# The FFN of a transformer and RWKV stack: products of split values against plain fp32 products

## The chip, the cores and the metric

The program runs on one core of one Trainium2 chip. The metric is the time on the device of one execution, in microseconds. The core has five engines with a program each: TensorE (PE), VectorE (DVE), ScalarE (ACT), GpSimd (POOL) and SyncE (SP, here only for DMAs). They run side by side and wait for each other on semaphores.

## The reference

Eight sequences of 1024 tokens with 256 channels go through four blocks, each with a layernorm before it and a residual after it: causal attention with rotary embedding, a gated FFN, an RWKV6 block, and the same FFN again. The FFN's weights are whole numbers from -127 to 127, scaled:

```python
x = x + _L0_attn_a_ref(_layernorm(x), Wq, Wk, Wv, Wo)
x = x + _L0_ffn_ref(_layernorm(x), w_gate, w_up, w_down)
x = x + _L0_attn_b_ref(_layernorm(x), ...)
x = x + _L0_ffn_ref(_layernorm(x), w_gate, w_up, w_down)
...
wg = w_gate.astype(x.dtype) * (1.0 / 127.0)
gate = jnp.einsum('bsd,hd->bsh', x, wg)
up = jnp.einsum('bsd,hd->bsh', x, wu)
h = jax.nn.silu(gate) * up
return jnp.einsum('bsh,dh->bsd', h, wd)
```

The hidden width is 768. All of it is fp32.

## The kernel before

A loop runs over the eight sequences (`b`, called batches here). In each, the stages follow one another: attention, first FFN (`ffn(1, ...)`, semaphore set 0), RWKV block, second FFN (`ffn(3, ...)`, set 1). Each engine has its own list, written out by hand, and each instruction is issued in that order. PSUM has eight banks; six of them (`RING`) are handed out in the order of one list, `psum_plan`, in which every product stands with the engine that empties its bank. `wait_bank` on PE waits until the product six places earlier has been emptied; `wait_filled` and `wait_emptied` are the waits of the other engines and of later steps.

An FFN works on halves `f` of 512 tokens and on tiles of 128 hidden rows: 12 tiles `e` for each sequence. For a tile, `gate_up` makes two products of 128x512 (`gu`, gate and up), each a sum over two chunks of 128 channels. ACT makes a tanh of the gate product (`turn`, L862), DVE adds one and multiplies by the gate (L1139) and then by the up product (L1144). `down` multiplies the hidden tiles by `wd` into 128x256 outputs, a sum over six tiles. Half of the down products stand in the middle of the tiles and half at the end.

The value operand of each product is split in two. `xh` is the input rounded to float32r, written by ACT (L846), and `xl` is the rest, written by DVE (L1126). In the same way `hh` is the rounded hidden tile, written by ACT (L853), and `hl` the rest, written by POOL (L683). PE takes both against the same float32r weights:

```python
for x in (xh, xl):
    w, v = wgu[:, c, rows], x[:, c, cols]
    last = mm(bank(b, f"gu{k}", 2 * e + r)[:, :], w, v, start=..., stop=...)
```

The hidden tiles stand in a ring: four places for `turn` (`TURNS`), ten or seven for `hh` and `hl` (`SLOTS`). The setup rounds the weights to float32r, subtracts that from the weights, and sets a flag if anything is left over (L504 to L516). PE loads it, and ahead of each FFN a branch chooses between these products and the same ones in plain fp32 (`general`).

Inside the first FFN stage PE also makes the second half of the attention's output projection (`out_proj(2)` and `out_proj(3)`, L1420) after tile 0, the transposes of the second half of the normed input (L1333), and at its end 16 transposes for what comes next. In the second, it makes four pieces of V for the next sequence (`v_item`, L1355) at the end.

Names: `xn` stands in the tile `attn`, `arena` is a large SBUF tile for most temporaries, `PB` are the PSUM banks. L1537 (`lora_item`) is the first product of the RWKV block; L1712 is its last one, L1525 its `mix` products.

Of the kernel before, what the change touches and what calls it, by code (L numbers as in the profile page):

```python
# [6 lines left out]
NB, T, D = 8, 1024, 256  # L7
# [56 lines left out]
SLOTS = {1: 10, 3: 7}  # L64
TURNS = 4
# [47 lines left out]
def psum_plan():  # L113
# [6 lines left out]
    def ffn(b, k):  # L120
        for f in (0, 1):
            for e in range(2 * NM):
                if f == 0 and k == 1 and e == 2:
                    add(b, "o", (2, 3), "dve")
                if f == 0 and e == 2 * SECOND_AT[k]:
                    add(b, f"ln{k}", (2, 3), "dve")
# [16 lines left out]
    for b in range(NB):  # L143
# [16 lines left out]
        add(b, "ln1", (0, 1), "dve")  # L160
# [47 lines left out]
        add(b, "ln3", (0, 1), "dve")  # L208
# [14 lines left out]
def build(nc, x_in, w_at, cs, b_vec, b_mat, ffn_w, consts, out):  # L223
    f32, bf16, i32, f32r = mybir.dt.float32, mybir.dt.bfloat16, mybir.dt.int32, mybir.dt.float32r
# [3 lines left out]
    with ctx:  # L228
# [19 lines left out]
        wgu = sb("wgu", [128, NC, 2 * HID], f32r)  # L248
        wd = sb("wd", [128, NM, D], f32r)
        wide_row = sb("wide_row", [128, 128])  # L250
        wide_flag = sb("wide_flag", [128, 1], i32)
# [39 lines left out]
        def rounded(name, first, shape):  # L291
            assert first + shape[1] * shape[2] <= ARENA
            return nc.alloc_sbuf_tensor_at(name, shape, f32r, offset=ARENA_AT + 4 * first)

# [16 lines left out]
        def ffn_tiles(k, first, hidden):  # L311
            return (rounded(f"xh{k}", first, [128, NC, T]), rounded(f"xl{k}", first + 2048, [128, NC, T]),
                    region(first + 4096, 512 * TURNS).rearrange("p (r t) -> p r t", r=TURNS),
                    rounded(f"hh{k}", hidden, [128, SLOTS[k], HALF]),
                    rounded(f"hl{k}", hidden + 512 * SLOTS[k], [128, SLOTS[k], HALF]))

        ffn_sets = {1: ffn_tiles(1, 0, 4096 + 512 * TURNS), 3: ffn_tiles(3, HIGH, HIGH + 4096 + 512 * TURNS)}
        assert HIGH + 4096 + 512 * (TURNS + 2 * SLOTS[3]) <= LAST

# [32 lines left out]
        s_split = sem("weights_split")  # L352
        s_raw = sem("raw_weights_moved")
        s_ones = sem("ones_stored")
        s_flag = sem("flag_moved")
# [31 lines left out]
        x_high = [sem("x_high1"), sem("x_high3")]  # L387
        h_high = [sem("h_high1"), sem("h_high3")]
        h_low = [sem("h_low1"), sem("h_low3")]
# [45 lines left out]
        NW = 2 * NC * HID + NM * D  # L435
        WF_AT, WR_AT, ONES_AT = 20 * 1024, 10 * 1024, 26 * 1024
        FLAG_AT = WF_AT - 1
        wf = arena[:, WF_AT:WF_AT + NW]
        gate, up = (wf[:, NC * HID * r:NC * HID * (r + 1)].rearrange("p (c n) -> p c n", c=NC) for r in (0, 1))
        down = wf[:, 2 * NC * HID:].rearrange("p (m n) -> p m n", m=NM)  # L440
        wr = rounded("wr", WR_AT, [128, 1, NW])
        ones = arena[96:99, ONES_AT:ONES_AT + 512].bitcast(bf16).rearrange("p (a n) -> p a n", a=1).broadcast_to([3, NH, T])
        with nc.Block() as block:
            @block.sync
            def _(sp):
# [32 lines left out]
                sp.wait_ge(s_split, 1)  # L478
                sp.dma_start(wgu[:, :, 0:HID].bitcast(f32), gate).then_inc(s_raw, 16)
                sp.dma_start(wgu[:, :, HID:2 * HID].bitcast(f32), up).then_inc(s_raw, 16)  # L480
                sp.dma_start(wd[:, :, :].bitcast(f32), down).then_inc(s_raw, 16)
                sp.wait_ge(s_split, 5)
                sp.dma_start(wide_row[0:1, :], arena[:, FLAG_AT:FLAG_AT + 1]).then_inc(s_flag, 16)
                sp.wait_ge(s_raw, 48)
# [15 lines left out]
            @block.vector  # L500
            def _(dve):
                dve.wait_ge(s_w, 16 * NLOAD)
                ai = arena[:, :].bitcast(i32)
                dve.tensor_copy(wf, ai[:, 0:NW]).then_inc(s_split, 1)  # L504
                dve.wait_ge(s_split, 1)
                dve.tensor_copy(wr[:, 0, :], wf).then_inc(s_split, 1)
                dve.wait_ge(s_split, 2)
                dve.tensor_tensor(arena[:, 0:NW], wf, wr[:, 0, :].bitcast(f32), ALU.subtract).then_inc(s_split, 1)
                dve.wait_ge(s_split, 3)
                dve.tensor_scalar(arena[:, 0:NW], arena[:, 0:NW], 0.0, None, ALU.not_equal).then_inc(s_split, 1)  # L510
                dve.wait_ge(s_split, 4)
                dve.reduce_max(arena[:, FLAG_AT:FLAG_AT + 1], arena[:, 0:NW], axis=AX.X).then_inc(s_split, 1)
                dve.wait_ge(s_flag, 16)
                dve.reduce_max(arena[0:1, WR_AT - 1:WR_AT], wide_row[0:1, :], axis=AX.X).then_inc(s_split, 1)
                dve.wait_ge(s_split, 6)
                dve.tensor_copy(wide_flag[0:1, :], arena[0:1, WR_AT - 1:WR_AT])  # L516
                dve.tensor_copy(causal[:, :], arena[:, 8192:8320])
                dve.tensor_copy(identb[:, :], ident[:, :]).then_inc(s_cast, 1)
# [22 lines left out]
        with nc.Block() as block:  # L541
# [49 lines left out]
            def _(pool):  # L591
# [22 lines left out]
                for b in range(NB):  # L614
# [65 lines left out]
                    def h_low_part(k, s, e):  # L680
                        _, _, turn, hh, hl = ffn_sets[k]
                        pool.wait_ge(h_high[s], 2 * NM * b + e + 1)
                        pool.tensor_tensor(hl[:, e % SLOTS[k], :], turn[:, e % TURNS, :], hh[:, e % SLOTS[k], :].bitcast(f32),  # L683
                                           ALU.subtract).then_inc(h_low[s], 1)
# [73 lines left out]
                    for e in range(2 * NM):  # L758
                        h_low_part(3, 1, e)

            @block.scalar
            def _(act):
# [27 lines left out]
                for b in range(NB):  # L790
# [48 lines left out]
                    def ffn(k, s):  # L839
                        xh, _, turn, hh, _ = ffn_sets[k]  # L840

                        def x_parts(ns):
                            for n in ns:
                                f, c = n // 2, n % 2
                                wait_filled(act, b, f"ln{k}", n)
                                act.activation(xh[:, c, HALF * f:HALF * f + HALF], bank(b, f"ln{k}", n)[:, :],  # L846
                                               ACT.Copy).then_inc(x_high[s], 1)

                        def h_part(e):
                            wait_emptied(act, b, f"gu{k}", 2 * e + 1)  # L850
                            if e >= SLOTS[k]:
                                wait_filled(act, b, f"dn{k}", 1)
                            act.activation(hh[:, e % SLOTS[k], :], turn[:, e % TURNS, :], ACT.Copy).then_inc(h_high[s], 1)  # L853

                        x_parts((0, 1))
                        for e in range(2 * NM):
                            if e == SECOND_AT[k]:
                                x_parts((2, 3))
                            wait_filled(act, b, f"gu{k}", 2 * e)
                            if e >= TURNS:  # L860
                                act.wait_ge(h_low[s], 2 * NM * b + e - TURNS + 1)
# [904 lines left out]
```

## Time and profile before

| | |
|---|---|
| time, median of three runs | 3376.86 us (3376.3 to 3377.62) |
| profiled execution | 3373.62 us |
| its span, first to last instruction | 3371.8 us |
| mean granted TensorE clock | 0.96 of full |
| PE, DVE, POOL, ACT busy | 87%, 71%, 42%, 39% of the span |
| share of the chain that ended last: PE, DVE, POOL | 51%, 23%, 12% |

Busy time of PE is the union of its records, and a record lasts until its result is out: the next one starts before it ends. So the length of a record is not what it costs in a row of them; that is the distance between starts. The chain is the work followed back from the last instruction.

### The profile page before, as it was taken

The page shows a single profiled execution, that of the slowest core. Times are in us where ns is not written, and L with a number is a line of the kernel's source. Part 1 is how long each engine was busy: PE and PEld are TensorE (multiplying, and loading weights), DVE is VectorE, ACT ScalarE, POOL GpSimd, SP SyncE. Part 2 cuts the span into 40 slices and gives each one's busy share as a digit, 9 for nine tenths or more (in the row PEclk, how much of TensorE's full clock was granted, in tenths as well). Part 3 has the DMA queues.
Part 4 walks back from the last instruction along what each step waited for, and adds up shares of the span by engine and source line. Part 5 has one row for each costly group of instructions (what it writes and reads, how often), then busy time and mean ns, then how long its engine had stood idle before and what let it go on. Part 6 is the DMA issues. An engine that isn't in the chain of part 4 may idle for free.

```text
span 3371.8 us, 47013 instructions
## 1 busy us (share of the span) xinstructions
PE 2943.3 (87%) x17088; PEld 1831.6 (54%) x17088; DVE 2399.7 (71%) x4593; ACT 1311.6 (39%) x2721; POOL 1413.6 (42%) x1596
## 2 busy tenths in 40 slices
PE   2398989989899898999989998898988989899898
PEld 1135565365653666445763457635575365654567
DVE  4485687767877677866778658785587756876666
ACT  0164314723246323453225532364313733247222
POOL 0123462335623356234552336423463334623454
PEclk9699999999999999999999999999999999999999
DMA  3700024000340004300051002500024000240000
GB/s 132 129 2 1 19 39 96 2 1 19 46 89 2 1 19 69 66 2 10 17 89 39 1 10 41 102 2 2 19 39 96 2 1 19 39 84 2 1 1 14
DMA packets 70610, 114.96 MB, mean 34 GB/s; under 512 B 9451, under 2 KB 62731, under 8 KB 64187
## 3 DMA queue, kind: packets, MB, share of 16 engines
q1 hardware_dynamic: 67091, 110.72, 16.8%
q8 instruction: 167, 2.74, 0.4%
q10 hardware_dynamic: 3264, 0.79, 0.1%
q14 instruction: 88, 0.72, 0.1%
HBM read 74.69 MB, written 33.65 MB: 32 GB/s over the span
## 4 chain that ended last, share of the span: by engine, by line
PE 51%; DVE 23%; POOL 12%; issue 5%; ACT 3%; DMA 3%; SPq 0%; DVEq 0%; POOLq 0%; ACTq 0%
PE PB L1411 7%; PE PB L1395 6%; PE PB L1381 6%; PE PB L1483 5%; PE PB L1468 5%; DVE mxp L1073 4%; DVE arena L1250 4%; PE PB L1420 3%; PE PB L1525 3%; DVE arena L1259 3%; DVE attn L995 2%; PE PB L1560 2%; POOL hl L683 2%; PE PB L1550 2%; DMA arena<-augT 2%
## 5 line engine op out<-in xcount | busy, mean ns | idle before, releaser
L1073 DVE TENSOR_REDUCE mxp<-PB 128x1 f32<-128x512 f32 (+3 forms) x1216 | 723.5, 652 | 149.3 <-PE PB L1384 96.1
L826 ACT ACTIVATE arena<-PB 128x512 f32<-128x512 f32 (+3 forms) x1536 | 657.6, 512 | 408.6 <-PE PB L1395 358.5
L1381 PE MATMUL PB<-arena 96*128 96x512 bf16 (+3 forms) x1536 | 463.2, 343 | 49.4 <-DMA arena<-parts 31.5
L1395 PE MATMUL PB<-arena 99*128 99x512 bf16 (+3 forms) x1536 | 444.1, 336 | 45.1 <-DMA arena<-augT 25.6
L683 POOL TENSOR_TENSOR hl<-arena,hh 128x512 fp32r<-128x512 f32 x192 | 251.8, 1311 | 357.0 <-ACT hh L853 354.0
L1468 PE MATMUL PB<-xh,wgu 128*128 128x512 f32 x768 | 317.1, 413 | 34.0 <-DVE xl L1126 18.4
L1411 PE MATMUL PB<-arena 128*32 128x512 f32 (+3 forms) x3072 | 325.6, 498 | 9.6 <-POOL arena L659 9.6
L1468 PE MATMUL PB<-xl,wgu 128*128 128x512 f32 x768 | 310.0, 404 | 0.6 <-issue 0.6
L1381 PEld LDWEIGHTS PB<-arena 96*128 96x128 bf16 x1536 | 151.6, 100 | 281.0 <-DVE mxp L1073 96.3
L659 POOL TENSOR_SCALAR_AFFINE_SELECT arena<-arena 128x512 f32<-128x512 f32 x256 | 162.4, 635 | 330.8 <-ACT arena L826 304.0
L703 POOL TENSOR_TENSOR arena<-arena,xT 128x512 f32<-128x512 f32 x160 | 184.2, 1175 | 261.8 <-DVE arena L1192 261.8
L1395 PEld LDWEIGHTS PB<-arena 99*128 99x128 bf16 x1536 | 139.2, 99 | 263.6 <-DVE mxp L1073 83.4
L1655 PE MATMUL PB<-arena 128*128 128x128 f32 x1792 | 240.8, 289 | 47.5 <-DVE arena L1250 39.2
L1655 PEld LDWEIGHTS PB<-arena 128*128 128x128 f32 x1792 | 222.4, 199 | 70.5 <-DVE arena L1250 54.1
L1483 PE MATMUL PB<-wd,hh 128*128 128x256 f32 x768 | 195.4, 296 | 66.5 <-POOL hl L683 66.5
L653 POOL TENSOR_TENSOR attn<-attn,sumT 128x512 f32<-128x512 f32 x64 | 81.2, 1269 | 343.3 <-DVE sumT L1088 343.3
L1192 DVE SCALAR_TENSOR_TENSOR arena<-PB,vec,arena 128x512 f32<-128x512 f32 x160 | 115.5, 746 | 149.1 <-PE PB L1525 147.4
L862 ACT ACTIVATE arena<-PB 128x512 f32<-128x512 f32 x192 | 114.2, 595 | 256.6 <-PE PB L1468 256.6
L726 POOL TENSOR_TENSOR arena<-arena 128x512 f32<-128x512 f32 x112 | 153.5, 1371 | 128.6 <-PE PB L1655 128.6
L1384 PE MATMUL PB<-causal,identb 128*128 128x128 bf16 x1024 | 204.0, 227 | 0.0
L1483 PEld LDWEIGHTS PB<-wd,hh 128*128 128x128 f32 x768 | 153.4, 200 | 79.2 <-DVE arena L1144 70.4
L1468 PEld LDWEIGHTS PB<-xh,wgu 128*128 128x128 f32 x768 | 149.1, 194 | 80.4 <-DVE xl L1126 23.0
(142 smaller groups left out, 5531.1 us busy)
## 6 DMA issues: line engine op xcount, KB each, us to landing
arena<-parts SPq DMA_DIRECT2D x112, 256.0 KB, 9.5
parts<-arena SPq DMA_DIRECT2D x192, 128.0 KB
arena<-parts SPq DMA_DIRECT2D x16, 768.0 KB, 17.4
arena<-in_x SPq DMA_DIRECT2D x16, 512.0 KB, 7.0
arena<-parts SPq DMA_DIRECT2D x16, 512.0 KB, 19.6
xres<-in_x SPq DMA_DIRECT2D x16, 512.0 KB, 4.6
out<-xres SPq DMA_DIRECT2D x16, 512.0 KB, 14.0
wgu<-arena SPq DMA_DIRECT2D x2, 768.0 KB, 4.5
```

What stands on the lines that cost most here:

```text
L659: pool.affine_select(out=a, in_=a, compare_op=ALU.is_ge, fill=0.0, base=0, pattern=[[0, HG], [1, 128]], channel_multiplier=-1).then_inc(ma ...
L683: pool.tensor_tensor(hl[:, e % SLOTS[k], :], turn[:, e % TURNS, :], hh[:, e % SLOTS[k], :].bitcast(f32), ALU.subtract).then_inc(h_low[s], 1)
L703: pool.tensor_tensor(a, a, xT[:, c, 1 + HALF * f:1 + HALF * f + HALF], ALU.add).then_inc(mix_added, 1)
L826: act.activation(pt[:, U % 3, h, 0:n], bank(b, "score", t)[:, 0:n], ACT.Exp, scale=DH ** -0.5).then_inc(act_emptied, 1)
L1073: dve.reduce_max(mxp[:, k // 2 % 2, hs[0]:hs[-1] + 1, col:col + 1], bank(b, "max", t)[:, 0:n * len(hs)].rearrange("p (h n) -> p h n", n=n) ...
L1381: last = mm(ps, qst[0:AUG, i // 4, HG * (k // 2) + h, 128 * (i % 4):128 * (i % 4) + 128], kst[0:AUG, s0 // HALF, HG * (k // 2) + h, 0:n], ...
L1384: last = mm(ps[:, n - 128:n], identb[:, :], causal[:, :], start=False, stop=True)
L1395: mm(ps[:, 0:n], kst[0:AUG + 3, j // 4, h, 128 * (j % 4):128 * (j % 4) + 128], qst[0:AUG + 3, f, h, HALF - n:HALF], start=True, stop=True) ...
L1411: last = mm(PB[6 + f][32 * h:32 * h + 32, t0 - HALF * f:HALF], vp[:, j, g * HG + h, :], pt[:, U % 3, h, 0:n], start=(j == 0), stop=(j == 4 ...
L1468: last = mm(bank(b, f"gu{k}", 2 * e + r)[:, :], w, v, start=(c == 0 and x is xh), stop=(c == NC - 1 and x is xl))
L1483: last = mm(bank(b, f"dn{k}", n)[:, D * a:D * a + D], v, w, start=(m == 0 and h is hh), stop=(m == NM - 1 and h is hl))
L1655: last = mm(bank(b, "level", n)[:, 128 * a:128 * a + 128].rearrange("p (h b m) -> p h b m", h=2, m=m), kk[:, c, 128 * ch:128 * ch + 128], ...
```

## The change

The split is taken out. `ffn_x` holds the input as it is and `ffn_h` all twelve hidden tiles, both fp32. ACT copies the transposed input to `ffn_x` and empties that bank itself; tanh and gate work in place in `ffn_h`; DVE's `x_low`, ACT's `h_part` and POOL's `h_low_part` are gone. The weights are fp32, cast straight from the integers. There is no flag, no branch and no second form of the FFN.

```diff
-        add(b, "ln1", (0, 1), "dve")
+        add(b, "ln1", (0, 1), "act")
...
-        wgu = sb("wgu", [128, NC, 2 * HID], f32r)
-        wd = sb("wd", [128, NM, D], f32r)
+        wgu = sb("wgu", [128, NC, 2 * HID])
+        wd = sb("wd", [128, NM, D])
...
+        ffn_x = {1: ct(region(0, 2048)), 3: ct(region(HIGH, 2048))}
+        ffn_h = {k: region(at, 512 * 2 * NM).rearrange("p (r t) -> p r t", r=2 * NM) for k, at in ((1, 10240), (3, HIGH + 4096))}
...
-                dve.tensor_copy(wf, ai[:, 0:NW]).then_inc(s_split, 1)
-                dve.wait_ge(s_split, 1)
-                dve.tensor_copy(wr[:, 0, :], wf).then_inc(s_split, 1)
...
+                for r in (0, 1):
+                    dve.tensor_copy(wgu[:, :, HID * r:HID * r + HID],
+                                    ai[:, 1536 * r:1536 * r + 1536].rearrange("p (c n) -> p c n", c=NC)).then_inc(s_cast, 1)
+                dve.tensor_copy(wd[:, :, :], ai[:, 3072:4608].rearrange("p (m n) -> p m n", m=NM)).then_inc(s_cast, 1)
...
-                    for e in range(2 * NM):
-                        h_low_part(1, 0, e)
-                        if e == 0:
-                            ln_scale(1, b, 1)
-                        if e == 8:
-                            ln_scale(2, b, 0)
+                    ln_scale(1, b, 1)
+                    ln_scale(2, b, 0)
...
-                                for x in (xh, xl):
-                                    w, v = wgu[:, c, rows], x[:, c, cols]
...
+                                if m == 0 and r == 0:
+                                    wait_emptied(pe, b, f"ln{k}", 2 * f + c)
+                                last = mm(bank(b, f"gu{k}", 2 * e + r)[:, :], wgu[:, c, rows],
+                                          ffn_x[k][:, c, HALF * f:HALF * f + HALF], start=(c == 0), stop=(c == NC - 1))
...
-                            pe.wait_ge(h_low[s], 2 * NM * b + NM * f + ms[-1] + 1)
+                            wait_emptied(pe, b, f"gu{k}", 2 * (NM * f + ms[-1]) + 1)
...
-                                for h in (hh, hl):
-                                    w, v = wd[:, m, :], h[:, (NM * f + m) % SLOTS[k], t]
...
+                                last = mm(bank(b, f"dn{k}", n)[:, D * a:D * a + D], ffn_h[k][:, NM * f + m, t], wd[:, m, :],
+                                          start=(m == 0), stop=(m == NM - 1))
...
-                    with pe.If_ne(wide, 0):
-                        ffn(1, 0, True)
-                    with pe.Else():
-                        ffn(1, 0, False)
+                    ffn(1)
```

On PE, at the entry of the first FFN stage, these rows stood (rows are an instruction with what it writes and reads; a count is that of instructions of the program):

```order
L1411 MATMUL PB<-arena 32x256 x4
L1411 MATMUL PB<-arena 32x128 x4
L1333 MATMUL PB<-ident,attn 128x128 x8
L1514 COMPARE_AND_BRANCH
L1468 MATMUL PB<-xh_49,wgu 128x512
L1468 MATMUL PB<-xl_50,wgu 128x512
```

Now, with the line numbers of the changed kernel:

```order
L1328 MATMUL PB<-arena 32x256 x4
L1328 MATMUL PB<-arena 32x128 x4
L1250 MATMUL PB<-ident,attn 128x128 x8
L1380 MATMUL PB<-arena,wgu 128x512 x4
L1337 MATMUL PB<-wo,attn 128x256 x16
L1380 MATMUL PB<-arena,wgu 128x512 x12
```

The branch has gone, and a tile has four gate and up matmuls instead of eight; the order of the products is the same.

On DVE, at the same place, before (L1083 to L1088 are the last softmax sums, L1139 and L1144 the gate of tile 0):

```order
L1083 STREAM_TRANSPOSE sumT<-attn 128x512
L1086 RECIPROCAL recip<-sumT 128x16
L1088 STREAM_TRANSPOSE sumT<-recip 128x512
L1126 TENSOR_TENSOR xl_50<-PB,xh_49 128x512 x2
L1139 SCALAR_TENSOR_TENSOR arena<-arena,PB 128x512
L1144 TENSOR_TENSOR arena<-PB,arena 128x512
```

And now:

```order
L1016 STREAM_TRANSPOSE sumT<-attn 128x512
L1019 RECIPROCAL recip<-sumT 128x16
L1021 STREAM_TRANSPOSE sumT<-recip 128x512
L1062 SCALAR_TENSOR_TENSOR arena<-arena,PB 128x512
L1067 TENSOR_TENSOR arena<-PB,arena 128x512
```

The two subtractions that stood between the sums and the first gate are out, and PE's first product no longer follows DVE.

On POOL, through the first FFN stage, before (L596 and L598 are the layernorm's scales):

```order
L653 TENSOR_TENSOR attn<-attn,sumT 128x4x128
L683 TENSOR_TENSOR hl_52<-arena,hh_51 128x512
L596 TENSOR_SCALAR mv<-mv 128x4
L598 TENSOR_TENSOR rstd<-mv,half_neg 128x4
L683 TENSOR_TENSOR hl_52<-arena,hh_51 128x512 x8
```

And now:

```order
L611 TENSOR_TENSOR attn<-attn,sumT 128x4x128
L554 TENSOR_SCALAR mv<-mv 128x4
L556 TENSOR_TENSOR rstd<-mv,half_neg 128x4
L554 TENSOR_SCALAR mv<-mv 128x4
L556 TENSOR_TENSOR rstd<-mv,half_neg 128x4
L641 MEMSET arena 64x2x1024
```

The twelve subtractions are out, and the scales follow one another without them.

## Rows read from the trace of the kernel before

**Rows 1.** the page, busy time and instructions of each engine

```profile
PE 2943.3 (87%) x17088; PEld 1831.6 (54%) x17088; DVE 2399.7 (71%) x4593; ACT 1311.6 (39%) x2721; POOL 1413.6 (42%) x1596
```

**Rows 2.** groups of PE, whole run, shapes apart: busy us, mean ns, idle before

```profile
L1468 PE MATMUL PB<-xh,wgu 128*128 128x512 f32 x768 | 317.1, 413 | 34.0 <-DVE xl L1126 18.4
...
L1483 PE MATMUL PB<-wd,hh 128*128 128x256 f32 x768 | 195.4, 296 | 66.5 <-POOL hl L683 66.5
...
L1346 PE MATMUL PB<-arena,wqkv 128*128 128x512 f32 x256 | 119.2, 606 | 1.4 <-ACT arena L766 1.4
...
L1355 PE MATMUL PB<-wqkv,arena 128*128 128x256 f32 x256 | 61.7, 391 | 0.0
```

**Rows 3.** windows, gate/up matmuls alone: PE busy (count), weight loads, granted clock, DMA

```profile
724.93:732.40 7.47, 7.47 (x32) 5.88 (x32) 1.00 0.00 0
```

**Rows 4.** windows, down matmuls alone, same columns

```profile
719.20:724.93 5.73, 5.73 (x48) 5.69 (x48) 1.00 0.02 4
```

**Rows 5.** PE timeline, other fp32 products: start us, length us, count

```profile
752.96 3.60 PE L1525 MATMUL PB<-arena,mw 128*128 128x512 f32 x8
...
943.54 3.61 PE L1355 MATMUL PB<-wqkv,arena 128*128 128x256 f32 x16
...
741.66 1.04 PE L1333 MATMUL PB<-ident,arena 128*128 128x128 f32 x8
```

**Rows 6.** PE timeline, first FFN stage of the second batch, waits in brackets

```profile
691.77 0.76 PE L1468 MATMUL PB<-xh,wgu 128*128 128x512 f32 x1 [2.96 <-DVE xl L1126]
...
709.46 1.65 PE L1333 MATMUL PB<-ident,attn 128*128 128x128 f32 x8 [0.86 <-DVE attn L995]
...
737.73 0.55 PE L1483 MATMUL PB<-wd,hh 128*128 128x256 f32 x1 [5.17 <-POOL hl L683]
...
747.70 0.70 PE L1537 MATMUL PB<-arena,mw 128*128 128x512 f32 x1 [0.94 <-DVE arena L1182]
```

**Rows 7.** windows of one stage of each FFN, all engines, granted clock

```profile
688.80:747.70 58.90, 48.30 (x249) 41.09 (x248) 32.83 (x64) 17.49 (x32) 19.96 (x18) 0.91 0.00 1
...
905.60:950.30 44.70, 39.71 (x218) 32.68 (x218) 29.43 (x48) 18.64 (x34) 19.81 (x16) 1.00 0.47 81
```

**Rows 8.** PE timeline, second FFN stage of the same batch

```profile
906.35 0.47 PE L1468 MATMUL PB<-xh,wgu 128*128 128x512 f32 x1 [0.74 <-DVE xres L1056]
...
911.74 1.42 PE L1333 MATMUL PB<-ident,attn 128*128 128x128 f32 x7 [0.95 <-DVE attn L995]
...
941.18 0.36 PE L1483 MATMUL PB<-wd,hh 128*128 128x256 f32 x1 [1.72 <-POOL hl L683]
```

**Rows 9.** windows at half clock inside the first FFN stage

```profile
689.80:696.70 6.90, 4.93 (x12) 3.91 (x13) 2.63 (x5) 0.60 (x1) 1.27 (x1) 0.51 0.01 2
...
737.60:741.10 3.50, 3.37 (x16) 3.40 (x17) 0.00 (x0) 0.03 (x1) 1.28 (x1) 0.51 0.00 0
```

**Rows 10.** timeline of ACT and DVE at the entry of the first FFN stage

```profile
688.40 1.08 ACT L846 ACTIVATE xh<-PB 128x512 fp32r<-128x512 f32 x2 [0.31 <-PE PB L1333]
...
689.80 1.25 DVE L1126 TENSOR_TENSOR xl<-PB,xh 128x512 fp32r<-128x512 f32 x2
```

**Rows 11.** groups of DVE, ACT and POOL instructions inside an FFN

```profile
L1139 DVE SCALAR_TENSOR_TENSOR arena<-arena,PB 128x512 f32<-128x512 f32 x192 | 130.2, 678 | 43.6 <-ACT arena L862 43.3
...
L862 ACT ACTIVATE arena<-PB 128x512 f32<-128x512 f32 x192 | 114.2, 595 | 256.6 <-PE PB L1468 256.6
...
L683 POOL TENSOR_TENSOR hl<-arena,hh 128x512 fp32r<-128x512 f32 x192 | 251.8, 1311 | 357.0 <-ACT hh L853 354.0
```

**Rows 12.** DVE timeline of the setup before the first batch

```profile
33.13 2.56 DVE L504 CAST arena<-arena 128x4608 f32<-128x4608 int32 x1 [33.13 <-DMA arena<-in_f_w_down]
...
53.35 0.21 DVE L518 CAST identb<-ident 128x128 bf16<-128x128 f32 x1
```

**Rows 13.** PE timeline around the FFN stage that ends the run

```profile
3327.90 1.89 PE L1712 MATMUL PB<-bm,xT 128*128 128x256 f32 x8
...
3367.34 0.28 PE L1483 MATMUL PB<-wd,hl 128*128 128x256 f32 x1
```

More of the change, by code:

```diff
@@ L63 @@
 V_AT = (4, 8)
-SLOTS = {1: 10, 3: 7}
-TURNS = 4
 NMAX = len(MAXES)
@@ L432, in wait_bank @@
                 eng.wait_ge(emptied[PLAN[n][1]], RANK[n])
[L435 to L441, printed above, removed]
+        ONES_AT = 26 * 1024
         ones = arena[96:99, ONES_AT:ONES_AT + 512].bitcast(bf16).rearrange("p (a n) -> p a n", a=1).broadcast_to([3, NH, T])
@@ L477, in _ @@
                 sp.dma_start(ones_dram, ones).then_inc(s_ones, 16)
[L478 to L484, printed above, removed]
                 sp.wait_ge(s_ones, 16)
@@ L757, in _ @@
                         turn_in(b + 1, 7)
-                    for e in range(2 * NM):
-                        h_low_part(3, 1, e)
             @block.scalar
@@ L1118, in _ @@
                         x0_norm(b + 1, 1)
-                    def x_low(k, s, ns):
-                        xh, xl, _, _, _ = ffn_sets[k]
-                        for n in ns:
-                            f, c = n // 2, n % 2
-                            cols = slice(HALF * f, HALF * f + HALF)
-                            dve.wait_ge(x_high[s], 4 * b + n + 1)
-                            dve.tensor_tensor(xl[:, c, cols], bank(b, f"ln{k}", n)[:, :], xh[:, c, cols].bitcast(f32),
-                                              ALU.subtract).then_inc(dve_emptied, 1)
                     dve.wait_ge(x_loaded[0], 16 * (b + 1))
@@ L1460, in gate_up @@
                             rows = slice(HID * r + 128 * m, HID * r + 128 * m + 128)
-                            cols = slice(HALF * f, HALF * f + HALF)
                             wait_bank(pe, b, f"gu{k}", 2 * e + r)
                             for c in range(NC):
-                                for x in (xh, xl):
-                                    w, v = wgu[:, c, rows], x[:, c, cols]
-                                    if general:
-                                        w, v = w.bitcast(f32), v.bitcast(f32)
-                                    last = mm(bank(b, f"gu{k}", 2 * e + r)[:, :], w, v,
-                                              start=(c == 0 and x is xh), stop=(c == NC - 1 and x is xl))
+                                if m == 0 and r == 0:
+                                    wait_emptied(pe, b, f"ln{k}", 2 * f + c)
+                                last = mm(bank(b, f"gu{k}", 2 * e + r)[:, :], wgu[:, c, rows],
+                                          ffn_x[k][:, c, HALF * f:HALF * f + HALF], start=(c == 0), stop=(c == NC - 1))
                             last.then_inc(filled, 1)
@@ L1716, in _ @@
                                 transpose_x(3, (0, 1))
-                    with pe.If_ne(wide, 0):
-                        ffn(3, 1, True)
-                    with pe.Else():
-                        ffn(3, 1, False)
+                    ffn(3)
 def kernel(**inputs):
```

82 lines of the change are left out of this document (12 added, 70 removed).

## The prediction, made before the changed kernel was run

> **What bounds the kernel now.** The first view is the page's busy times: PE has 87% of the span and DVE 71% [rows 1]. That is an average over four kinds of stage, so the next view is windows of one FFN stage of each kind. In the first FFN stage of the second batch, from the end of the input's transposes at 688.80 to the first RWKV product at 747.70 (58.9 us), PE is busy 48.3, DVE 32.8, POOL 20.0 and ACT 17.5 us. In the second FFN stage, from 905.60 to 950.30 (44.7 us), PE is busy 39.7, DVE 29.4, POOL 19.8, ACT 18.6 us [rows 7]. PE bounds both, with waits in between, and the question is what PE's products cost in each form and which waits go.
>
> PE's waits stand in its timeline. In the first FFN: 2.96 us for `xl` at the entry, 0.86 for the layernorm, 5.17 for POOL's `hl` ahead of the last down products, 0.94 at the way out [rows 6]. In the second: 0.74, 0.95, 1.72 [rows 8] and some shorter ones.
>
> **What a product costs.** Records overlap, so I count distances. Split form: 32 gate/up records take 7.47 us, 0.233 each; I use 0.231 (starts in the middle of that run are 0.23 apart) [rows 3]. 48 down records take 5.73 us, 0.119 each [rows 4]. Plain fp32 stands in the trace already, with the same shapes. First its number of records: `qk_item` has 128 matmuls in the program (8 batches, 8 items, 2 chunks) and 256 records at L1346, so a plain fp32 matmul leaves two records, while L1468 and L1483 leave one for each [rows 2]. Then their distance: eight 512-column records of L1525 take 3.60 us; less one record's own length, 0.61, that is seven steps of 0.428; I take 0.429. Sixteen 256-column records of L1355 take 3.61 us; less 0.39, fifteen steps of 0.215 [rows 2, 5]. So a 512-column matmul is 0.858 plain and a split pair 0.462; for 256 columns, 0.430 against 0.238.
>
> **The sum for PE.** A stage has 48 gate/up and 48 down matmuls of whole values, 96 records of each kind in either form. Gate/up: 96 x 0.231 = 22.2 becomes 96 x 0.429 = 41.2 us. Down: 96 x 0.119 = 11.4 becomes 96 x 0.215 = 20.6 us. That is 28.2 us a stage more, 451 us over 16 stages, if nothing came back.
>
> **What comes back.** In the changed FFN a tile keeps PE for 8 x 0.429 = 3.43 us. DVE needs two instructions of about 0.68 for it, ACT one of 0.60, and POOL's subtraction of 1.31 is gone [rows 11]. Even DVE's whole work in the first stage, 32.8 us less four subtractions, is under half of PE's. So every wait inside the stages should vanish, and I compute each stage as PE's work alone:
> - First FFN: 41.2 + 20.6, output projection 32 records of 256 columns x 0.215 = 6.9, transposes 24 at 0.109 = 2.6 (eight take 1.04 less the last one's overhang [rows 5]); in sum 71.3. At the entry PE now follows ACT's copy of the first chunk alone. The two copies run from 688.40 to 689.48, the subtractions until 691.05 [rows 10]; so PE starts at 689.1 instead of 691.77, 0.3 after the window's start. 71.6 against 58.9: +12.7, eight times, +101.6 us.
> - Second FFN: 41.2 + 20.6, transposes 0.9, V 16 x 0.215 = 3.4, in sum 66.1 against 44.7: +21.4, seven times, +150 us. It needs no wait for the transposes: the two tiles ahead of them now last 6.9 us, from 905.6 to 912.5, and the last of them began at 911.74 before. DVE's and ACT's rotary work for the next batch lies beside tiles that are 3.43 us long.
> - The last second FFN, without V: from 3329.79 to 3367.62, 37.8 us [rows 13], becomes 41.2 + 20.6 + 0.9 + 0.2 for the last result = 62.9: +25.1.
>
> The stage sums of before (22.2 + 11.4 + 6.9 + 2.6 = 43.1 of 58.9) leave 15.8 us in the first FFN, more than the 9.9 of waits: half clock is the rest. Between 689.8 and 696.7 and between 737.6 and 741.1 the granted clock is 0.51, the lower level of 1.2 GHz, each time after or in a stretch in which PE waited [rows 9]; half of 10.4 us is lost, 5.2. The second of these followed the 5.17 us wait and goes with it. Of the first a piece may stay, since the stretch ahead of it holds a wait for POOL and transposes that don't change: from nothing to one stretch like the second, 3.5 us at half, 1.7 us a batch. I take the middle, 0.85 x 8 = +7; both ends stay for the range.
>
> **Setup.** DVE starts at 33.13, when the last weight has landed, and ends at 53.56 [rows 12]. The cast of 4608 columns took 2.56; three of 1536 are 2.6 to 3.0 together, then two small ones of 0.2. The setup ends at about 36.3 instead: -17.3, all on the path, since every engine waits for its end. The branches cost some tenths at each entry, which the windows' ends hold already. Fewer instructions of ACT and POOL are worth nothing: they waited, POOL for ACT's `hh` 354 us in all and ACT's tanh for PE 257 us [rows 11].
>
> **The sum.** 101.6 + 150 + 25.1 + 7 - 17.3 = +266. The profiled execution took 3373.6 us; the median of the runs is 3.3 above it. 3376.9 + 266 = 3643 us.
>
> **Where the skill bears on it.** The rows show two records at 0.429 for one plain 512-column product [rows 2, 5]. The Trainium skill, Perfetto Trace Analysis, Engine Utilization, puts TensorE's output rate in its low/high fp32 form at half of the usual one; FP8 and Floating Point Precision, TensorE Precision Notes, has true fp32 take four passes. By the first, applied to a whole product, the change would gain; by the second it costs what the rows say. The two agree only if half rate is that of one record and a product has two, which is how the counts read.
>
> **The rivals.**
> - *A plain product costs one record, not two* (ends on the other side). One mechanism, in PE's array: a 512-column product 0.429, a 256-column one 0.215. A stage then needs 20.6 + 10.3 = 30.9 where it had 33.6, and the waits still go: first FFN 40.7 against 58.9, second 35.2 against 44.7, last 32.0 against 37.8. -146 - 66 - 6 - 17 + 7 = -228: 3149 us. It decides from 41% of the forecast rise on: the rise is 451, and what comes back with the setup is 185, so below records of about 0.31 us the kernel would be faster. Against it: the counts of L1346 and L1355. For it only that no row has this very line in plain form. 3 in 100. The rule on the output rate named above would give this outcome if it were meant for a whole product; the trace does not agree with that reading.
> - *The change costs nothing, as another engine covers it* (within 0.2%). PE would need 28 us of slack a stage; the waits in the windows are 15.8 and about 7. 1 in 100.
> - *Half clock comes more often.* The mean clock of 0.96 says that stretches at the lower level occur in other stages as well. The FFNs get longer, so later stages may meet them otherwise; two more stretches of 3.5 us a batch cost 3.5 x 8 = 28, on top of the upper end of my clock term: some 3680 to 3710. 8 in 100.
> - *Waits stay although PE is slower*: say, the entry of the stages or the ends still wait on DVE or ACT. All of them kept (9.9 x 8 + 3.4 x 8) would be +106, 3750. Against: the tile's 3.43 against 1.4. 4 in 100.
> - *More comes back*: half-clock stretches elsewhere fall away, or the RWKV stage starts with its inputs ready and gains more than its 0.94. One stretch of each stage gone is 1.7 x 16 = 27, and the clock term at zero: 3575 to 3610. 7 in 100.
>
> **How the numbers follow.** The forecast has 77 in 100. Its own bounds are: clock term -7 or +7, half-clock stretches elsewhere one a batch less or more (14), the steps of 0.429 and 0.215 to half a per cent (5), waits of some tenths at the new places (up to 1 us a stage, +16). That gives 3608 to 3685, with little outside but the rivals. Faster by over 0.2%, about what a measurement can tell here, needs the first rival: 0.03; within 0.2%: 0.01; slower: 0.96.
>
> **What the changed profile would show.** Gate/up and down should have 1536 records each as before, 0.429 and 0.215 apart, PE busy about 3340 us (23 and 26 us a stage more than [rows 7]). The waits for POOL on the down line (66.5 us before [rows 2]) and the 5.17 us wait should be gone. The first FFN window should be about 71.6 us and the second about 66. DVE's setup should end near 36. The prediction is wrong if the distances differ from those of L1525 and L1355, if the down products wait for the gates, or if a stage next to the FFNs changes its length by more than a few microseconds.

## The result, and the profile after

The changed kernel takes 3646.85 us (median of four runs, 3642.16 to 3649.99) against 3377.11 us before (median of four; the 3376.86 above is that of three): a ratio of 1.0798, with a 95% interval of 1.0779 to 1.0817. The forecast was 3643 us. A second series gave 3649.81 us (five runs).

The page of the changed kernel, busy times and clock:

```profile
PE 3343.8 (92%) x17088; PEld 1918.3 (53%) x17088; DVE 2345.8 (64%) x4525; ACT 1209.4 (33%) x2529; POOL 1164.9 (32%) x1404
...
PEclk8799999999999999999999999999999999999999
```

PE has as many records as before [rows 1] and 400 us more of busy time; DVE, ACT and POOL have less. The chain that ended last says the same by engine: PE was 51% of it and is now 66%, POOL went from 12% to 10%.

```profile
PE 66%; DVE 15%; POOL 10%; issue 4%; DMA 2%; ACT 2%; SPq 0%; DVEq 0%; POOLq 0%; ACTq 0%
```

The line has each engine's share of the chain. The groups of PE instructions, shapes apart (busy us, mean ns of one, idle before):

```profile
L1380 PE MATMUL PB<-arena,wgu 128*128 128x512 f32 x1536 | 675.3, 597 | 2.7 <-ACT arena L790 2.7
L1391 PE MATMUL PB<-wd,arena 128*128 128x256 f32 x1536 | 339.2, 379 | 0.0
```

These two answer to L1468 and L1483 [rows 2]. The 768 matmuls of each kind in the program leave 1536 records, two each. Ahead of the down products PE waited 66.5 us for POOL; now nothing. Ahead of gate/up 34 us have become 2.7, the wait for ACT's copy at the entries.

The PE timeline of the first FFN stage of the second batch (start, length, count, waits in brackets), which answers to [rows 6]:

```profile
708.80 4.51 PE L1380 MATMUL PB<-arena,wgu 128*128 128x512 f32 x6 [0.34 <-ACT arena L790]
...
756.18 13.90 PE L1380 MATMUL PB<-arena,wgu 128*128 128x512 f32 x32
769.92 4.48 PE L1391 MATMUL PB<-wd,arena 128*128 128x256 f32 x20
774.23 1.04 PE L1250 MATMUL PB<-ident,arena 128*128 128x128 f32 x8
775.11 1.04 PE L1250 MATMUL PB<-ident,attn 128*128 128x128 f32 x8
775.98 6.21 PE L1391 MATMUL PB<-wd,arena 128*128 128x256 f32 x28
```

One wait of 0.34 us is left in the stage. The distances: 13.90 us less one record of 0.60, over 31 steps, is 0.429; 6.21 less 0.38, over 27, is 0.216. The windows of a stage of each kind, and of the RWKV block between them, answer to [rows 7]:

```profile
708.50:782.10 73.60, 73.30 (x249) 45.83 (x250) 30.75 (x61) 10.96 (x20) 3.66 (x5) 0.98 0.00 1
942.10:1009.40 67.30, 67.30 (x217) 40.54 (x216) 28.31 (x46) 12.39 (x22) 3.72 (x4) 0.98 0.46 80
782.10:941.90 159.80, 142.66 (x713) 95.18 (x712) 119.61 (x233) 39.00 (x70) 95.16 (x78) 0.99 0.17 30
```

But for that wait PE is busy through the whole stage in both FFNs. Each of the two stages holds a stretch at half clock (3.4 and 2.4 us): four other first FFNs take 71.9 us and six other second ones 66.1. The setup on DVE, which answers to [rows 12]:

```profile
32.66 1.83 DVE L472 CAST wgu<-arena 128x1536 f32<-128x1536 int32 x2 [32.66 <-DMA arena<-in_f_w_down]
34.40 0.95 DVE L474 CAST wd<-arena 128x1536 f32<-128x1536 int32 x1
35.27 0.22 DVE L475 CAST causal<-arena 128x128 bf16<-128x128 f32 x1
35.41 0.22 DVE L476 CAST identb<-ident 128x128 bf16<-128x128 f32 x1
```

It ends at 35.6 us where it ended at 53.6.

I cut both traces at the FFNs: a stage goes from the end of PE's last record before its first gate/up record to the start of the next other record after its last down record. The 0.94 us before the RWKV block's first product thus counts to the first FFN. Summed over the eight batches of the profiled executions, without the 4.2 us behind PE's last record:

| us | before | after | difference | forecast |
|---|---|---|---|---|
| to PE's first matmul | 61.2 | 43.6 | -17.6 | -17.3 |
| first FFN | 468.6 | 579.2 | +110.6 | +101.6, and +7 for the clock |
| second FFN | 350.9 | 526.6 | +175.7 | +175.1 |
| attention | 1234.5 | 1233.3 | -1.2 | 0 |
| RWKV block | 1252.4 | 1261.4 | +9.0 | 0 |
| span | 3371.8 | 3648.2 | +276.4 | +266 |

The profiled execution of the changed kernel (3649.99 us) is the longest of its four, and that of the kernel before (3373.62 us) lies below its four, so the spans differ by more than the medians, which are 270 us apart. In the second series of the changed kernel, whose profiled span is 3643.3 us, the RWKV block is at 1257.9 and the first FFN at 577.5.

### The profile page after: what moved, and what is told of

Same layout as the page of the kernel before. It is cut to its first block, busy times and chain, and to the rows that moved or that the text cites. A ratio compares the mean times of both kernels' runs of the same rounds, so it can differ in the third digit from the quotient of the medians.

```text
span 3648.2 us, 46355 instructions
## 1 busy us (share of the span) xinstructions
PE 3343.8 (92%) x17088; PEld 1918.3 (53%) x17088; DVE 2345.8 (64%) x4525; ACT 1209.4 (33%) x2529; POOL 1164.9 (32%) x1404
## 4 chain that ended last, share of the span: by engine, by line
PE 66%; DVE 15%; POOL 10%; issue 4%; DMA 2%; ACT 2%; SPq 0%; DVEq 0%; POOLq 0%; ACTq 0%
PE PB L1380 18%; PE PB L1391 9%; PE PB L1298 6%; PE PB L1328 6%; PE PB L1312 6%; DVE mxp L1006 4%; DVE arena L1171 3%; PE PB L1337 3%; PE PB L1428 3%; DVE arena L1180 2%; PE PB L1463 2%; PE PB L1453 2%; PE PB L1272 1%; POOL arena L660 1%; ACT arena L772 1%
## 5 line engine op out<-in xcount | busy, mean ns | idle before, releaser
L1380 PE MATMUL PB<-arena,wgu 128*128 128x512 f32 x1536 | 675.3, 597 | 2.7 <-ACT arena L790 2.7
L1312 PE MATMUL PB<-arena 99*128 99x512 bf16 (+3 forms) x1536 | 443.7, 335 | 44.2 <-DMA arena<-augT 24.4
L1380 PEld LDWEIGHTS PB<-arena,wgu 128*128 128x128 f32 x1536 | 292.4, 192 | 350.8 <-issue 340.6
L1391 PE MATMUL PB<-wd,arena 128*128 128x256 f32 x1536 | 339.2, 379 | 0.0
L1391 PEld LDWEIGHTS PB<-wd,arena 128*128 128x128 f32 x1536 | 291.0, 190 | 53.1 <-issue 12.0
L1062 DVE SCALAR_TENSOR_TENSOR arena<-arena,PB 128x512 f32<-128x512 f32 x192 | 131.8, 687 | 226.2 <-ACT arena L798 225.9
L1558 PEld LDWEIGHTS PB<-arena 128*128 128x128 f32 x1792 | 213.3, 192 | 84.4 <-DVE arena L1171 66.5
L991 DVE SCALAR_TENSOR_TENSOR xres<-PB,xres 128x512 f32<-128x512 f32 x64 | 44.2, 691 | 239.2 <-PE PB L1391 239.2
```

The source lines that it names most:

```text
L1312: mm(ps[:, 0:n], kst[0:AUG + 3, j // 4, h, 128 * (j % 4):128 * (j % 4) + 128], qst[0:AUG + 3, f, h, HALF - n:HALF], start=True, stop=True) ...
L1380: last = mm(bank(b, f"gu{k}", 2 * e + r)[:, :], wgu[:, c, rows], ffn_x[k][:, c, HALF * f:HALF * f + HALF], start=(c == 0), stop=(c == NC - 1))
L1391: last = mm(bank(b, f"dn{k}", n)[:, D * a:D * a + D], ffn_h[k][:, NM * f + m, t], wd[:, m, :], start=(m == 0), stop=(m == NM - 1))
L1558: last = mm(bank(b, "level", n)[:, 128 * a:128 * a + 128].rearrange("p (h b m) -> p h b m", h=2, m=m), kk[:, c, 128 * ch:128 * ch + 128], ...
```

## The experiments

**The price of the product.** The kernel before holds a form of its FFN with every matmul in plain fp32. Here it is always taken, with the short setup of the changed kernel (below) and no branches; the splits and all their waits stay.

```diff
-                    with pe.If_ne(wide, 0):
-                        ffn(1, 0, True)
-                    with pe.Else():
-                        ffn(1, 0, False)
+                    ffn(1, 0, True)
```

> The kernel with the short setup and no branches, and the split kept whole (xh, xl, hh, hl and all their waits), but every matmul of the FFN in plain fp32, which is the form that the kernel before holds for wide weights. If the cost of the change is two records at 0.429 and 0.215 for each plain matmul, a stage's PE work rises from 33.6 to 96 x 0.858 + 96 x 0.430 = 123.7 us: 1441 us over 16 stages, less some 110 us of waits that go: 4690 us (4660 to 4720). Rival, the cost is one of switching to undivided values and not of the matmul form: near 3650 us.

Measured: 4674.42 us (two runs), ratio 1.3849 (1.3821 to 1.3877). Its groups on PE:

```profile
L1450 PE MATMUL PB<-xh,wgu 128*128 128x512 f32 x1536 | 798.2, 602 | 18.4 <-DVE xl L1110 18.4
L1450 PE MATMUL PB<-xl,wgu 128*128 128x512 f32 x1536 | 792.3, 598 | 0.0
```

The same instructions left 768 records for each part in float32r [rows 2]; in plain fp32 they leave 1536. The form alone, with nothing else of the change, costs 1318 us over the kernel with the short setup, 1441 less what waits and clock give back; that is inside the 4660 to 4720 us expected. So the price belongs to the matmul's form, and it scales with the count.

**PE's products halved instead.** One float32r product in place of each plain one, on the changed kernel's structure:

```diff
-        wgu = sb("wgu", [128, NC, 2 * HID])
+        wgu = sb("wgu", [128, NC, 2 * HID], f32r)
...
+        ffn_r = {k: rounded(f"fr{k}", at, [128, 2 * NM, HALF]) for k, at in ((1, 10240), (3, HIGH + 4096))}
```

> The changed kernel with one float32r product in place of each plain fp32 one: input, hidden tiles and weights are rounded to float32r and the rests are left out, so the output has less precision. PE's FFN work falls to 96 records a stage in all, 48 x 0.231 + 48 x 0.119 = 16.8 us where the changed kernel has 61.8; everything else of the changed kernel stays. Theory: with PE this light DVE bounds the FFN: about 45 us for the first FFN and 35 for the second, near 3170 us. Rival, PE bounds even this: 26.6 and 21.3 us, 2940 us. Rival, the change's loss is not PE's products but the new chain of copies and gates: the time stays above 3377 us.

Measured: 3184.08 us (two runs), ratio 0.9427 (0.9408 to 0.9446). The waits of PE name the next bound:

```profile
PE PB L1317 <- DMA arena<-augT: 70.8, 16, 24.0
PE PB L1255 <- DVE attn L933: 50.2, 38, 3.0
...
PE PB L1396 <- DVE arena L1067: 30.8, 14, 3.9
PE PB L1385 <- DVE arena L1067: 19.5, 22, 1.1
```

The columns are us in total, times and longest. In the FFNs PE waits for DVE's norms and gates. The structure of the changed kernel isn't slow; with PE this light DVE sets the stage, at 41.7 and 35.1 us against the 45 and 35 expected. That the time comes within 14 us of the 3170 expected is partly luck: the first FFNs are shorter than expected by 29 us in all, and the attention, which follows the now shorter second FFN, is longer by 37 than in the changed kernel (1270.5 against 1233.3); its wait for the DMA of `augT` is 70.8 us in this run and 24.4 in the changed kernel. The run also bounds what the rests cost: without them, and with the short setup, the time is 6% under the kernel before, with less precision in the output.

**Each side alone.** Both have the short setup and no branches. `gate_plain` takes gate/up whole and keeps `hh` and `hl`; `down_plain` takes the hidden tiles whole and keeps `xh` and `xl`.

```diff
-                                for x in (xh, xl):
...
+                                last = mm(bank(b, f"gu{k}", 2 * e + r)[:, :], wgu[:, c, rows], xh[:, c, cols],
+                                          start=(c == 0), stop=(c == NC - 1))
```

> The kernel with the short setup and no branches, and of the change only the gate/up side: input whole and in plain fp32, hidden tiles still split (hh by ACT, hl by POOL) for the down products. PE: 96 x (0.429 - 0.231) x 16 stages = +304 us. Back comes the wait for xl (2.3 us), the layernorm's and POOL's waits that a 3.43 us tile covers, and the half clock behind them: about 12 us in the first FFN, 3.5 in the second. Theory: 3357 + 304 - 125 = about 3530 us (3505 to 3545). Rival, the rise of the change is in the down products: under 3450 us.

```diff
-                                for h in (hh, hl):
...
+                                last = mm(bank(b, f"dn{k}", n)[:, D * a:D * a + D], turn[:, NM * f + m, t], wd[:, m, :],
+                                          start=(m == 0), stop=(m == NM - 1))
```

> The kernel with the short setup and no branches, and of the change only the down side: hidden tiles whole and in plain fp32, input still split (xh by ACT, xl by DVE) for gate and up. PE: 96 x (0.215 - 0.119) x 16 = +147 us. Back comes what PE waited for POOL's hl, as far as DVE's gates are done by then: some 3.5 us a stage of both kinds, and the half clock behind the longest. Theory: 3357 + 147 - 50 = about 3450 us (3435 to 3465). With the gate side's rise the two should come to less than the change's 290 us over the short setup, since each alone gets the shared waits back. Rival, down products cost nothing more because weights are loaded as often as before: 3310 us.

Measured: gate side 3522.54 us, 1.0440 (1.0423 to 1.0458), inside its expectation; down side 3412.40 us, 1.0110 (1.0093 to 1.0127). Over the 3356.88 us of the short setup they are +166 and +56; the change, with both, is +290. As expected the two come to less than the whole, since each alone gets back waits that the whole can get back but once. The down side beat its expectation by 38 us. The step that was off is what comes back in the first FFN. The expectation gave back 50 us in all, some 3.5 us a stage of both kinds less what DVE's gates hold back, and some clock. Of the waits for the gates ahead of the last down products the trace shows this:

```profile
PE PB L1447 <- DVE arena L1109: 6.4, 7, 1.0
```

Seven waits of 1.0 us at most. In the first FFN the down side took 466.8 us over eight stages, as good as the 466.5 of the short setup: the 9.2 us a stage more of PE's work were paid in full. PE's waits in these stages fell from 79.3 to 25.2 us in all (the 47.9 for `hl` went, 6.9 for the gates came, and some 7 each for the layernorm and at the way out went too), and the time at half clock, of which half is lost, from 99 to 51 us. In the second FFN the sums are 403.1 against 350.4.

**Branches and setup.**

```diff
-                    with pe.If_ne(wide, 0):
-                        ffn(1, 0, True)
-                    with pe.Else():
-                        ffn(1, 0, False)
+                    ffn(1, 0, False)
```

> The kernel before without the branch ahead of each FFN; split float32r products, flag and setup are kept (the flag is still computed and loaded, and nobody looks at it). My theory: a branch costs PE some tenths of a microsecond at each of 16 entries, 0.74 us of idle at the second FFN's entry and about 0.7 us behind the end of xl at the first's, so about 0.65 x 16 = 10 us less than before: 3367 us. Rival: at the first FFN the wait for xl covers the branch, and only the second gains: 3371 us. Rival: the branch costs nothing that PE does not lose to its bank waits anyway: 3377 us.

Measured: 3373.94 us (ten runs, 3372.93 to 3376.39), ratio 0.9990 (0.9980 to 0.9999). That is 3 to 4 us, not 10. The timeline of the second FFN of the second batch tells why:

```profile
907.88 0.99 PE L1468 MATMUL PB<-xh,wgu 128*128 128x512 f32 x1
908.67 0.63 PE L1468 MATMUL PB<-xl,wgu 128*128 128x512 f32 x1
909.09 0.63 PE L1468 MATMUL PB<-xh,wgu 128*128 128x512 f32 x1
...
914.58 1.42 PE L1333 MATMUL PB<-ident,attn 128*128 128x128 f32 x7 [0.95 <-DVE attn L995]
```

The 0.74 us at the entry [rows 8] is gone, but the first records are 0.42 apart, not 0.23: in the window 907.88 to 911.20 the granted clock is 0.56, where the same place had 1.00 before. And the transposes wait 0.95 us for DVE's norm as before, which would have taken in the gain in any case. At the first FFN the wait for `xl` is 2.30 instead of 2.96 us. Over eight batches the first FFN became 3.5 us shorter and the second no shorter, and in all second FFNs together 18.1 us ran at half clock, where it had been 2.3. The two profiled executions don't show the gain as a whole: the RWKV block is 3.4 and the attention 1.9 us longer in the one without branches, whose span is 1.6 us over that of the kernel before. So the 3 to 4 us stand on the medians alone.

Then the setup (same edit, and the DVE casts of the change into float32r weights, without the flag):

```diff
-                dve.tensor_copy(wf, ai[:, 0:NW]).then_inc(s_split, 1)
...
+                for r in (0, 1):
+                    dve.tensor_copy(wgu[:, :, HID * r:HID * r + HID],
+                                    ai[:, 1536 * r:1536 * r + 1536].rearrange("p (c n) -> p c n", c=NC)).then_inc(s_cast, 1)
```

> The kernel before without branches, and with the setup of the changed kernel: integers are cast straight to the float32r weights, no flag, no check for wide integers. Products stay split. Theory: the setup ends 17.3 us earlier and all of it is on the path: 17 us less than the run without branches, about 3350 us. Rival: the first loads of the batches take the place of the setup and half of it is lost: 3358 us.

Measured: 3356.88 us, ratio 0.9938 (0.9921 to 0.9955): 17.1 us under the run without branches, all of it on the path. (The expected 3350 us had the 10 us of the branches in it.)

**Cover for the waits.** In the split kernel the last waits of a stage can be covered instead of removed: PE makes its transposes or V ahead of the last down products.

```diff
-                        for n in (2, 3):
-                            down(n, 0, range(NM - 1))
                         if k == 1:
...
                             v_item(b + 1, 1)
+                        for n in (2, 3):
+                            down(n, 0, range(NM - 1))
```

> As the kernel with the short setup and no branches, and at the end of each FFN PE makes the 16 transposes (first FFN) or V (second) ahead of the last down products and not between them. Theory: the waits for POOL's hl there, 5.17 us and 1.72 us, come while PE has 1.75 and 3.4 us of other work, so 1.75 and 1.7 us a stage come back, and some of the half clock behind the 5.17 us wait: 26 to 40 us less than the kernel with the short setup, 3310 to 3324 us. Rival: the transposes' inputs are not ready at that point and nothing is gained: 3350 us.

> The changed kernel with the transposes and V ahead of the last down products, as in the turned end. The trace of the changed kernel has no idle time of PE ahead of its down products, so there is nothing to cover: 3647 us, within 4 us. Rival, that hidden waits between records of the changed kernel still hold 1 us or more a stage: 3630 us or less. The turned end gained 25 us on the split kernel.

Measured: split kernel 3332.22 us, ratio 0.9868 (0.9851 to 0.9884), 25 us under the short setup; changed kernel 3646.28 us, no difference from 3646.85. The same edit is worth 25 us where PE waits and nothing where it doesn't. In the split kernel the waits for `hl` went from 67.2 us with the short setup to 24.9:

```profile
PE PB L1465 <- POOL hl L667: 24.9, 24, 2.7
```

At 25 us it is just under the 26 to 40 expected: the transposes now have a wait of their own, 1.74 us for DVE's gate, and attention and RWKV block grew by some 7 us each. In the attention the wait for the DMA of `augT` grew, from 28.1 to 42.6 us.

**Where the 0.94 us went.** In the changed kernel the RWKV block's first product no longer waits, yet the block isn't shorter. Its PE timeline:

```profile
782.02 3.60 PE L1440 MATMUL PB<-arena,mw 128*128 128x512 f32 x8
...
794.32 1.93 PE L1453 MATMUL PB<-arena,low 128*64 128x512 f32 x4 [0.96 <-POOL arena L651]
```

The same place before:

```profile
759.32 1.07 PE L1550 MATMUL PB<-arena,low 128*64 128x512 f32 x2 [0.18 <-POOL arena L703]
```

The wait for POOL's additions grew by 0.78 us. POOL behind the FFN:

```profile
782.25 1.80 POOL L641 MEMSET arena<- 64x2048 f32 x1 [22.60 <-PE PB L1391]
784.11 1.80 POOL L643 MEMSET arena<- 64x2048 f32 x1
786.00 0.20 POOL L554 TENSOR_SCALAR mv<-mv 128x4 f32<-128x4 f32 x1
786.28 1.01 POOL L556 TENSOR_TENSOR rstd<-mv,half_neg 128x4 f32<-128x4 f32 x1
```

Two clearings stand ahead of the layernorm's scale, for which DVE waits. I moved the scale between them, with a repeat of the changed kernel beside it:

```diff
+                    ln_scale(2, b, 1)
+                    pool.wait_ge(ln_rstd[2], 2 * b + 2)
                     pool.memset(qd[64:128, :, 0, :], 0.0).then_inc(qd_zeroed, 1)
                     pool.wait_ge(qd_zeroed, 2 * b + 2)
-                    ln_scale(2, b, 1)
```

> The changed kernel once more, unaltered, as the yardstick on this chip for the run with the earlier scale. 3642 to 3650 us, as before.

> The changed kernel, and on POOL behind the first FFN the layernorm's scale for the second half stands between the two clearings of qd (1.80 us each), not behind both. In the changed kernel PE starts the RWKV block 0.94 us sooner after its last down product than before, and then waits 0.96 us for POOL's additions at the first product of the decay branch; the chain to it runs over the two clearings, the scale, DVE's norm, rotary and first mix. Theory: that wait is where the 0.94 us went, the earlier scale takes 1.8 us out of the chain and the wait goes: 0.96 x 8 = 7 to 8 us less than the changed kernel, and the RWKV block from 159.5 to 158.6 us on average. Rival: another wait stands right behind it (POOL's clearing then delays ACT's copies of r), no difference.

> The kernel with the short setup, no branches and the turned end, and the earlier scale. The turned end took 27 us out of the first FFN stages and 13 out of the second, but the RWKV block grew by 6.8 us in all and the attention by 7. Theory: as in the changed kernel the RWKV block's part is the wait for POOL behind the clearings; 6 to 10 us less than the 3332 us of the turned end, 3322 to 3326 us. Rival: the growth is half clock in those stages and not the wait: 3332 us.

Measured: the change again 3649.81 us (3645.07 to 3652.75), with the earlier scale 3644.35 (3642.4 to 3645.69), and the turned end with it 3329.90 (3326.48 to 3332.54), ratio 0.9861 (0.9846 to 0.9876). The turned end with it is 2 us faster than without, not 6 to 10, and that is inside the spread of the runs. The gap of 5 us in the changed kernel isn't the wait: that went only from 7.5 to 6.3 us, and the profiled executions of the two differ by 0.7 us. What makes the gap stays open. The trace of the earlier scale, first POOL, then DVE:

```profile
785.90 1.80 POOL L645 MEMSET arena<- 64x2048 f32 x1
```

```profile
785.95 2.86 DVE L929 TENSOR_SCALAR attn<-xres,mv,rstd 128x256 f32<-128x256 f32 x4 [1.56 <-POOL rstd L556]
```

DVE's norms began 1.4 us sooner but ran beside the clearing, and the four took 2.86 us, against 1.38 in the kernel before and after. The slowdown isn't even. The lengths of the four, shortest, median and longest, in ns:

```profile
L929 DVE TENSOR_SCALAR attn<-xres,mv,rstd x4: 395/400/1900, 786.0 to 788.4; 128x256 f32<-128x256 f32 x4
```

The first norm lasts 1.90 us instead of 0.41, to the end of the clearing (787.70), and the other three run at their usual pace behind it; it is so in all eight batches. The Trainium skill, GPSIMD Engine Reference, Key points, says that POOL shares its SBUF interfaces with DVE, and that they contend when DVE runs in its two-port mode or takes two inputs from SBUF. The trace agrees that they contend; which mode the norm ran in it doesn't show. So in the last run the second clearing waits for the norms as well:

```diff
                     pool.wait_ge(ln_rstd[2], 2 * b + 2)
+                    pool.wait_ge(ln_out[2], 8 * (b + 1))
                     pool.memset(qd[64:128, :, 0, :], 0.0).then_inc(qd_zeroed, 1)
```

> As the run with the earlier scale, but the second clearing of qd also waits until DVE's four norms are done. With the scale first alone, rstd came 1.4 us earlier, but the clearing then ran beside DVE's norms, four of which took 2.86 us and not 1.38, and the first mix on DVE began where it had begun before. Theory: with the clearing out of DVE's way the norms take 1.38 us again, DVE's first mix begins 1.4 us earlier, and PE's wait for POOL's additions, 0.96 us, goes to nothing: the waits of that line from 7.5 us to under 1, and 7 us less than the changed kernel's 3650 on this chip, 3643 us. Rival: the mix product of PE itself sets DVE's start, the wait stays at 0.8 us, and the time with it at 3644 to 3650 us.

Its waits and its norms:

```profile
PE PB L1455 <- POOL arena L653: 0.4, 1, 0.4
```

```profile
784.36 1.38 DVE L930 TENSOR_SCALAR attn<-xres,mv,rstd 128x256 f32<-128x256 f32 x4 [1.56 <-POOL rstd L556]
```

Measured: 3643.36 us (3634.78 to 3647.19), on another chip, against 3649.81 (3645.07 to 3652.75). The wait is gone, as the theory has it, and the medians differ by 6.4 us; but the runs of both spread by as much, the first series of the unaltered kernel has 3646.85 us, and the RWKV block's sum, 1257.3 us, is hardly shorter than the repeat's 1257.9. That the chain over clearing, scale and norm makes the wait is shown; that removing it makes the kernel faster is not shown.

## Why the prediction was right

- **Records and distances.** Two records to a plain product, 0.429 and 0.215 us apart: measured 0.429 and 0.216. That the rows of other lines, with the same shapes and types, carried over to a line that had not yet run is what the forecast rested on, and `split_in_plain` shows the same price with the rest unchanged. The rival of one record is out, and with it the reading for a whole product of the output rate in the Trainium skill, Perfetto Trace Analysis, Engine Utilization.
- **What comes back.** The stage was computed as PE's work alone: 71.6 and 66.1 us. The stages measured 71.9 and 66.1; three of eight first FFNs take 73.6 and one of seven second ones 67.3, each with a stretch at half clock. (The forecast took all eight first FFNs of before at 58.9 us; the first and the last of them are 57.7 and 57.1, and their sum is 2.6 us less than it counts with.) The other engines' relief was worth nothing by itself, as `high_only` shows from the other side: they matter once PE has a third of the work.
- **Clock.** The three long stages hold the term that I put between 0 and 14 us. In the window of one of them:

```profile
709.00:712.40 3.40, 3.40 (x5) 1.34 (x5) 0.53 (x1) 0.15 (x1) 1.26 (x1) 0.50 0.02 5
```

  Half clock at the entry, after the unchanged wait for POOL and the transposes, and 1.7 us lost; three times 1.7 is 5, against the 7 taken. The mean granted clock went from 0.960 to 0.976. Most of that is in the first FFNs, where 81.9 us ran at half clock before and 10.2 after; it went together with PE's waits there, as the prediction has it. In all, 274 us ran at half clock before and 180 after, so the rival in which it comes more often is out.
- **Setup.** -17.3 forecast, -17.6 measured, -17.1 when done alone.
- **What was off.** The RWKV block was put at no change and grew by 9.0 us in this trace (5.5 in the repeat's). Two waits of PE in it grew: that for POOL's additions from 1.9 to 7.5 us in all, and this one, for DVE (before, then after):

```profile
PE PB L1655 <- DVE arena L1250: 39.2, 58, 1.4
...
PE PB L1558 <- DVE arena L1171: 48.3, 70, 1.4
```

  I had counted the 0.94 us at the block's first product as gained for good, and most of it was given back twelve microseconds later. How much of the 9.0 us that is, the single blocks tell. Windows over the fifth and the sixth of the changed kernel:

```profile
2109.70:2269.40 159.70, 142.58 (x714) 95.22 (x713) 119.58 (x233) 39.01 (x70) 95.13 (x78) 0.99 0.18 30
2551.60:2710.00 158.40, 143.35 (x714) 96.56 (x713) 118.60 (x233) 39.00 (x70) 94.72 (x78) 0.98 0.18 31
```

  The sixth has its two stretches of half clock where the blocks before have theirs, some 83 and 154 us behind its start, and takes 158.4 us against 157.9: so the longer wait for POOL costs 0.5 us a block, an estimate of 4 us in all. The fifth, and the four others that take 159.3 to 160.1 us, have only one stretch, 155 to 156 us behind the start. Without the one at 83 us PE gains nothing, for it waits 7.2 us for DVE's L1171 in place of 5.7. That the rest of the growth goes with the place of the last stretch is what the blocks show; why it falls there stays open. The branches were counted in the windows' ends; alone they are worth 3 us, not the 10 of my expectation. All of this is small beside 266 us, but that the forecast lies within 4 us of the median is closer than its terms are: in the profiled executions the rise is 10 us above it.
- **The range.** Its lower end, 3608 us, is 9 us below what its own terms give (3643 less 7, 14 and 5 is 3617). Nothing hangs on it here.

The fastest of the kernels tried that keep the precision is the split one with the short setup, no branches, the turned end and the earlier scale: 3329.90 us, 1.4% under the kernel before. It is no better than the same without the earlier scale by more than the runs' spread. It leaves out the form for wide integers.

## What to carry to other kernels

Price a matmul by the distance between starts in the rows of the same type and shape, and by records to a matmul of the program; the mean lengths of a record (0.41 and 0.60 us here) differ by a factor of 1.5 where the distances differ by 1.9. When PE gets heavier in a stage where it waits, write the stage as PE's work alone and give the waits back once, not once for each cause. And follow a gained microsecond to the next chain: the next engine's list may hold it.

## What was unexpected of the hardware

- A float32r record of 512 columns is 0.231 us behind the last, a bit more than half of a plain fp32 record's 0.429; for 256 columns it is 0.119 against 0.216. A plain product makes two such records, so high and rest parts in float32r cost 54% of one plain product (0.462 to 0.858 us).
- Four norms on DVE took 2.86 us beside a POOL clearing and 1.38 without it. All of the loss is in the first, which lasts until the clearing ends (1.90 us instead of 0.41), while the clearing takes 1.80 us as ever.
- With 0.7 us of idle time at each entry taken out of PE's program, the stretches of half clock lay elsewhere in the profiled execution: the first records of the second FFN ran at 0.56 where they had run at 1.00. A gain of a few tenths a stage can vanish in that.
